# A recurrent block's GLA projections: fp32 products replaced by three fp16 products, with the weights split on POOL

## The reference

```python
xn = rmsnorm(x, ln1_w)                 # x is already layer-normed
q = xn @ Wq                            # 256 -> 128
k = xn @ Wk * scaling                  # 256 -> 128
gk = log_sigmoid(xn @ Wkg1 @ Wkg2 + bkg2) / 16   # 256 -> 16 -> 128
v = xn @ Wv                            # 256 -> 256
g = xn @ Wg + bg                       # 256 -> 256
...                                    # scan over tokens: S = S*exp(gk) + k v ; o = q S
x = x + (silu(g) * norm(o)) @ Wo
```

## Time and profile before

| | |
|---|---|
| median of three runs | 1288.07 us (1287.93 to 1289.17) |
| the profiled execution | 1286.95 us |
| its span in the profile | 1285.2 us |
| PE busy | 1127.8 us (88%) |
| DVE busy | 917.3 us (71%) |
| ACT busy | 691.5 us (54%) |
| POOL busy | 439.1 us (34%) |

### The profile page before, as it was taken

The page is one execution under the profiler, slowest core; times in us unless marked ns, Lnnn a source line. Parts: engine busy times, 40 slices in busy tenths (PEclk is TensorE's granted clock), DMA queues, the critical chain, the costliest instruction groups (busy, mean ns, idle before and its releaser), DMA issues. The chain is left out here.

```text
span 1285.2 us, 20632 instructions
## 1 busy us (share of the span) xinstructions
PE 1127.8 (88%) x6922; PEld 638.0 (50%) x6922; DVE 917.3 (71%) x1500; ACT 691.5 (54%) x1217; POOL 439.1 (34%) x253
## 2 busy tenths in 40 slices
PE   6866988999999899999997879756779999999997
PEld 4455855555555555555553754422344544444443
DVE  4978159999999899999995154799634155655554
ACT  3554267888777787777884124500554044344443
POOL 2821054444444354444220004254420033333331
PEclk9965988999999999999998987898879999999999
DMA  5243018887777787777779010400000344444331
GB/s 157 78 132 113 1 33 138 143 143 142 138 140 141 132 144 144 144 141 140 133 137 213 2 41 1 125 1 0 1 1 1 78 112 118 114 121 122 117 118 49
DMA packets 332820, 126.79 MB, mean 99 GB/s; under 512 B 273296, under 2 KB 328064, under 8 KB 332736
## 3 DMA queue, kind: packets, MB, share of 16 engines
q1 hardware_dynamic: 332736, 125.72, 45.6%
HBM read 57.26 MB, written 1.31 MB: 46 GB/s over the span
## 5 line engine op out<-in xcount | busy, mean ns | idle before, releaser
L1067 DVE SCALAR_TENSOR_TENSOR a_pr<-a_ex,a_rtot,a_pr 128x1024 f16<-128x1024 f32 x128 | 206.4, 1613 | 3.7 <-ACT a_pr L992 3.6
L848 POOL TENSOR_TENSOR a_rnorm<-a_ss,a_power 128x8 f32<-128x8 f32 x32 | 80.2, 2508 | 258.4 <-DVE a_ss L1033 258.3
L2058 POOL TENSOR_TENSOR e_sg<-e_sg,e_cb 128x512 f32<-128x512 f32 x64 | 82.0, 1282 | 242.1 <-ACT e_sg L2006 242.1
L1054 DVE TENSOR_REDUCE a_nmax<-psum 128x1 f32<-128x1024 f32 x128 | 155.4, 1214 | 12.9 <-PE psum L907 9.2
L984 ACT ACTIVATE a_ex<-psum,a_nmax 128x1024 f32<-128x1024 f32 x128 | 142.8, 1116 | 12.4 <-DVE a_nmax L1054 8.9
L992 ACT ACTIVATE a_pr<-a_ex,a_rtot 128x1024 f16<-128x1024 f32 x128 | 147.4, 1152 | 0.0
L889 PE MATMUL psum<-a_wh,xT_h 128*128 128x128 f16 (+1 forms) x512 | 115.3, 248 | 3.8 <-PEq L578 1.2
L2014 ACT ACTIVATE e_hh<-e_hf 128x512 f16<-128x512 f32 x64 | 40.3, 630 | 143.4 <-DVE e_hf L2083 143.4
L890 PE MATMUL psum<-a_wl,xT_h 128*128 128x128 f16 (+1 forms) x512 | 115.1, 248 | 0.0
L891 PE MATMUL psum<-a_wh,xT_l 128*128 128x128 f16 (+1 forms) x512 | 115.1, 248 | 0.0
L921 PE MATMUL psum<-a_pT,a_vh 128*128 128x512 f16 x256 | 98.2, 384 | 7.6 <-DMA a_pT<-a_pr 7.6
(11 more groups left out here) (349 smaller groups left out, 2706.8 us busy)
## 6 DMA issues: line engine op xcount, KB each, us to landing
e_cb<-comb_by_expert SPq DMA_DIRECT2D x64, 256.0 KB, 3.8
wf<-in_L_ffn_W_gate SPq DMA_DIRECT2D x32, 128.0 KB, 2.4
wf<-in_L_ffn_W_up SPq DMA_DIRECT2D x32, 128.0 KB, 2.4
wf<-in_L_ffn_W_down SPq DMA_DIRECT2D x32, 128.0 KB, 2.8
e_guf<-in_L_ffn_wg SPq DMA_DIRECT2D x32, 128.0 KB, 2.3
e_guf<-in_L_ffn_wu SPq DMA_DIRECT2D x32, 128.0 KB, 2.3
e_dnf<-in_L_ffn_wd SPq DMA_DIRECT2D x32, 128.0 KB, 2.1
a_wf<-in_L_attn_wq SPq DMA_DIRECT2D x16, 128.0 KB, 3.0
```

The lines of the kernel that those rows point to most:

```text
L1054: dve.tensor_reduce(nmax[:, k:k + 1], score_banks(m), AX.X, ALU.max, negate=True).then_inc(max_ready, 1)
L1067: dve.scalar_tensor_tensor(pr[k][:, 1, :], ex[e][:, :], rtot[:, e:e + 1], pr[k][:, 0, :], ALU.mult, ALU.subtract).then_inc(p_ready, 1)
```

## The change

The five projection weights are split into fp16 halves by POOL, in the block of the first norm (`side=split_weights`). For each weight POOL waits for its load, multiplies it by 64 in place, casts the high half and subtracts it to get the low half; `wv` is permuted in the same steps, chunk by chunk, which takes the place of L1508. The second norm now makes `xT_h` and `xT_l`. PE makes three fp16 products in place of each fp32 product of `wg1`, `wq`, `wk`, `wv` and `wg`, and waits for POOL's counts instead of the loads. The second gate product, the router's logits and all turns stay fp32. ACT and DVE divide by 64 where they read the sums.

```diff
-            xT = ptmp("xT", [P, DC, T])
+            xT_h, xT_l = ptmp("xT_h", [P, DC, T], F16), ptmp("xT_l", [P, DC, T], F16)
...
+            def split_weights(pool):
+
+                order = (("wg1", wg1, 2), ("wq", wq, 0), ("wk", wk, 1), ("wv", wv, 3), ("wg", wg, 4))
+                scaled = at = 0
+                for name, whole, i in order:
+                    pool.wait_ge(w_loaded[i], 16)
+                    high, low = halves[name]
+                    views = [(whole[:, :, :], high[:, :, :], low[:, :, :])]
+                    if name == "wv":
+                        views = [(whole[:, c, :].rearrange("p (h c d) -> p c d h", c=2, d=8),
+                                  *(x[:, c, :].rearrange("p (c d h) -> p c d h", c=2, d=8) for x in (high, low))) for c in range(DC)]
+                    scaled += 1
+                    pool.tensor_scalar(whole[:, :, :], whole[:, :, :], WSCALE, None, ALU.mult).then_inc(w_scaled, 1)
+                    pool.wait_ge(w_scaled, scaled)
+                    for f, h, l in views:
+                        at += 1
+                        pool.tensor_copy(h, f).then_inc(w_high, 1)
+                        pool.wait_ge(w_high, at)
+                        pool.tensor_tensor(l, f, h, ALU.subtract).then_inc(w_low, 1)
...
-            layer_norm(nc, env, "ln1", env["x"], xn, env["xnT"], interleaved=True, loads=load_first, stats=env["x1_stats"],
+            layer_norm(nc, env, "ln1", env["x"], xn, env["xnT"], interleaved=True, loads=load_first, stats=env["x1_stats"], side=split_weights,
...
-            rms_turned("g1_r1", xn, 0, xT, loads=load_rest)
+            rms_turned("g1_r1", xn, 0, xT_h, xT_l, loads=load_rest)
...
                     for c in range(DC):
-                        last = pe.matmul(psum[0:rows, banks + half, :], lhs(c), rhs_of(c, half),
-                                         start=(c == 0), stop=(c == DC - 1))
+                        pe.matmul(bank, wh[:, c, cols], xT_h[:, c, tokens], start=(c == 0), stop=False)
+                        pe.matmul(bank, wh[:, c, cols], xT_l[:, c, tokens], start=False, stop=False)
+                        last = pe.matmul(bank, wl[:, c, cols], xT_h[:, c, tokens], start=False, stop=(c == DC - 1))
...
-                    for i in range(len(loads) + 1):
-                        pe.wait_ge(w_loaded[i], 16)
+                    pe.wait_ge(w_loaded[5], 16)
+                    pe.wait_ge(w_low, 1)
...
-                    pool.wait_ge(w_loaded[3], 16)
-                    for c in range(DC):
-                        pool.tensor_copy(wv_dh[:, c, :].rearrange("p (c d h) -> p c d h", c=2, d=8),
-                                         wv[:, c, :].rearrange("p (h c d) -> p c d h", c=2, d=8)).then_inc(wv_ready, 1)
...
-                        dve.tensor_tensor(silu_g[:, n, :], psum[:, 4 + n % 2, 0:D], bg[:, :], ALU.add).then_inc(g_added, 1)
+                        dve.scalar_tensor_tensor(silu_g[:, n, :], psum[:, 4 + n % 2, 0:D], 1.0 / WSCALE, bg[:, :], ALU.mult, ALU.add).then_inc(g_added, 1)
```

More of the change, by code:

```diff
@@ L1428, in gated_linear_attention @@
             wv, wg, bg = ptmp("wv", [P, DC, D]), ptmp("wg", [P, DC, D]), ptmp("bg", [P, D])
-            wv_dh = ptmp("wv_dh", [P, DC, D])
-            wv_ready = sem("g1_wv")
+            halves = {name: [ptmp(f"{name}_{part}", [P, DC, width], F16) for part in "hl"]
+                      for name, width in (("wg1", G1), ("wq", KD), ("wk", KD), ("wv", D), ("wg", D))}
+            w_scaled, w_high, w_low = sem("g1_ws"), sem("g1_wh"), sem("g1_wv")
             loads = [(wq, w["L1_attn_Wq"]), (wk, w["L1_attn_Wk"]), (wg1, w["L1_attn_Wkg1"]), (wv, w["L1_attn_Wv"]),
@@ L1455, in gated_linear_attention, with both @@
             qk_done, act_done, dve_done, vh_done, g_added, v_free, x_high = (sem("g1_" + s) for s in ("qd", "ad", "dd", "vh", "ga", "vf", "xh"))
-            def both(pe, banks, lhs, rhs_of, rows=P):
+            def both(pe, banks, name, cols, rows=P):
+                wh, wl = halves[name]
                 for half in range(2):
+                    tokens, bank = slice(half * HALF, (half + 1) * HALF), psum[0:rows, banks + half, :]
                     for c in range(DC):
-                        last = pe.matmul(psum[0:rows, banks + half, :], lhs(c), rhs_of(c, half),
-                                         start=(c == 0), stop=(c == DC - 1))
+                        pe.matmul(bank, wh[:, c, cols], xT_h[:, c, tokens], start=(c == 0), stop=False)
+                        pe.matmul(bank, wh[:, c, cols], xT_l[:, c, tokens], start=False, stop=False)
+                        last = pe.matmul(bank, wl[:, c, cols], xT_h[:, c, tokens], start=False, stop=(c == DC - 1))
                 return last
@@ L1471, in _ @@
                     router.make_logits(pe)
-                    for i in range(len(loads) + 1):
-                        pe.wait_ge(w_loaded[i], 16)
[L1475 to L1479, removed]
+                    pe.wait_ge(w_loaded[5], 16)
+                    pe.wait_ge(w_low, 1)
+                    both(pe, 0, "wg1", slice(0, G1), G1).then_inc(mid_ready, 1)
+                    pe.wait_ge(w_low, 2)
+                    both(pe, 2, "wq", slice(0, KD)).then_inc(q_ready, 1)
+                    pe.wait_ge(w_low, 3)
+                    both(pe, 4, "wk", slice(0, KD)).then_inc(q_ready, 1)
                     pe.wait_ge(mid_done, 1)
@@ L1487, in _ @@
                     pe.wait_ge(qk_done, 1)
-                    pe.wait_ge(wv_ready, DC)
+                    pe.wait_ge(w_low, 3 + DC)
                     for cv in range(2):
-                        both(pe, 2 * cv, lambda c: wv_dh[:, c, cv * P:(cv + 1) * P], x_of).then_inc(v_ready, 1)
+                        both(pe, 2 * cv, "wv", slice(cv * P, (cv + 1) * P)).then_inc(v_ready, 1)
                     for n in range(NT):
@@ L1493, in _ @@
                             pe.wait_ge(qk_done, 2)
+                            pe.wait_ge(w_low, 4 + DC)
                         if n >= 2:
                             pe.wait_ge(g_added, n - 1)
+                        (wh, wl), tokens = halves["wg"], slice(n * P, (n + 1) * P)
                         for c in range(DC):
-                            last = pe.matmul(psum[:, 4 + n % 2, 0:D], xT[:, c, n * P:(n + 1) * P], wg[:, c, :],
-                                             start=(c == 0), stop=(c == DC - 1))
+                            pe.matmul(psum[:, 4 + n % 2, 0:D], xT_h[:, c, tokens], wh[:, c, :], start=(c == 0), stop=False)
+                            pe.matmul(psum[:, 4 + n % 2, 0:D], xT_h[:, c, tokens], wl[:, c, :], start=False, stop=False)
+                            last = pe.matmul(psum[:, 4 + n % 2, 0:D], xT_l[:, c, tokens], wh[:, c, :],
+                                             start=False, stop=(c == DC - 1))
                         last.then_inc(g_ready, 1)
@@ L1523, in _ @@
                     act.wait_ge(mid_ready, 1)
-                    act.activation(mid[:, :], psum[0:G1, 0:2, :].rearrange("p a b -> p (a b)"), ACT.Copy).then_inc(mid_done, 1)
+                    act.activation(mid[:, :], psum[0:G1, 0:2, :].rearrange("p a b -> p (a b)"), ACT.Copy,
+                                   scale=1.0 / WSCALE).then_inc(mid_done, 1)
                     act.wait_ge(q_ready, 1)
-                    act.activation(qT[:, :], two(2), ACT.Copy).then_inc(qk_done, 1)
+                    act.activation(qT[:, :], two(2), ACT.Copy, scale=1.0 / WSCALE).then_inc(qk_done, 1)
                     act.wait_ge(q_ready, 2)
-                    act.activation(kT[:, :], two(4), ACT.Copy, scale=float(GV) ** -0.5).then_inc(qk_done, 1)
+                    act.activation(kT[:, :], two(4), ACT.Copy, scale=float(GV) ** -0.5 / WSCALE).then_inc(qk_done, 1)
                     router.exponentials(act)
@@ L1540, in _ @@
                         act.wait_ge(v_ready, cv + 1)
-                        act.activation(v_h[:, cv, :], two(2 * cv), ACT.Copy).then_inc(vh_done, 1)
+                        act.activation(v_h[:, cv, :], two(2 * cv), ACT.Copy, scale=1.0 / WSCALE).then_inc(vh_done, 1)
                     router.turned(act)
```

2 lines of the change are left out of this document (1 added, 1 removed).

## The result

The kernel after takes 1294.27 us in the median of six runs (1291.89 to 1295.53), the kernel before 1288.0 in six runs beside it. The ratio is 1.0043 with a 95% interval of 1.003 to 1.0056, so the change costs 5.5 us (3.9 to 7.2). The forecast said 4.6 and slower, so sign and size were right. One of its terms was too small by 2.7, and an error of the other sign in another hid 0.7 of that.

The account below looks back on a forecast made before the run. It took PE to bound the projections, with each block's end a meeting of engines, so stage times add. First norm +6.0, second norm +2.8 and projections -4.2 gave +4.6 us, forecast 1292.7 us, range 1290.0 to 1296.3.

Parts of the forecast that it names:

- First norm: First norm's block: its end now waits for POOL, done at 774.0, so the next block starts 6.0 us later.
- it has one input, and I take that line: POOL's multiplications in the first norm's block: priced as one-input instructions, 0.18 us + 0.83 per thousand elements.
- my upper bound, the two-input price: First norm's block: five multiplications at the two-input price (+1.7) and waits twice as long give 8.5 us.
- rival 4: First norm's block: POOL slower than its rows, by the upper bound or collisions; sum 7.1, 1295.2 us; chance 10%.
- The collision that the prediction allowed for: First norm's block: at most one POOL instruction collides with DVE's scaling (L166), 0.3 us, inside the bounds.
- The exclusion that the prediction names: First norm's block: a single-input DVE instruction of this kind and a POOL instruction exclude each other; sum 0.3 higher.
- Second norm: Second norm ahead of the projections: making both halves lengthens the stretch from 7.05 to 9.89 us, +2.8.
- DVE joins the turn: Second norm ahead of the projections: with halves DVE takes part in the turn, +2.8 us, bounds 2.6 and 3.0.
- Projections: Projections' block: PE's own gain from fp16 products is 6.4 us, of which 4.2 arrives; bounds -6.4 and -2.5.
- The stall: Third tile of wg in the projections: PE waits about 2.1 us, once, for DVE's first bias addition.
- rival 2: Projections: the clock falls in PE's new wait, last tiles of wg at half pace, +1.7, 1294.4 us; chance 15%.
- Rivals 1, 3 and 5: In order: POOL not last in first norm, 1286.7, 8%; no wg wait, 1290.5, 5%; projection products no cheaper, 1297, 2%.

Follow-up runs that it names:

- the masks last: Kernel after with wk, wv, wg split later, four banks in both second norms, two biases first; POOL makes router halves before head masks: ratio 0.9951, 1280.86 us.
- two biases first: Kernel after, with DVE adding the first two biases of wg ahead of its step of the gate's chain: ratio 1.0053 against the kernel before, 1294.4 us.

## Why the prediction was right, and where it was not

**First norm, +8.66 against +6.0.** The mechanism held, point by point. POOL began 4.19 us after the block's start, against 4.05 by my rows, and the block ended with it. The failed step is "it has one input, and I take that line". The five multiplications took 0.38 + 0.85 + 0.85 + 1.49 + 1.49 = 5.06 us where I had 2.23, which is +2.83. Everything else came to its price: the six casts 2.82 against 2.82, the six subtractions 4.31 against 4.5, the gaps 0.63 against 0.6, the meeting 0.36 against 0.5. Even my upper bound, the two-input price, was too low (1.16 for 512 elements against 1.49), so the block's +8.66 lies above the bound of 8.5. This is rival 4, "POOL is slower than its rows", with a chance of 10%, and its sum of 7.1 is nearer to the 6.58 of the profile than the forecast's 4.6. Waits had no part in it, and a collision at most 0.2 us. The four permuted instructions took 0.60 and 0.78, and again 0.60 and 0.79, together 2.77, against my 2.9. The rule of the Trainium skill (GPSIMD Engine Reference, Performance pitfalls for Q7 kernels) had given 3.2: the subtractions come out near its 0.8, the casts lie 0.2 below it. What the casts do bear out is the step between its two figures, one cycle per element, 0.21 us for 256 elements as an estimate: they took 0.20 more than the plain cast's 0.40. The subtractions took only 0.11 more than a plain one's 0.67.

The collision that the prediction allowed for, up to 0.3 us, does show, on POOL's side. POOL's first multiplication began 0.21 us before DVE's scaling (L166) ended and itself ended 0.17 after it (766.11 + 0.38 against 763.65 + 2.67). In the nine profiles that have this pair it took 0.38 to 0.50 us and always ended 0.15 to 0.17 after L166. By the line through 0.85 and 1.49 it would take 0.29, an estimate, so the collision is worth 0.1 us here and 0.2 at most. The exclusion that the prediction names agrees with that. L166 takes 2.67 us for eight tiles in both kernels.

**Second norm, +2.84 against +2.8.** Taking it whole from the later norm gave the right number. "DVE joins the turn" holds for two banks only; with four the stage took 6.70, as the experiment showed.

**Projections, -4.92 against -4.2.** `wq` and `wk` took 5.28 (from 800.88 to 806.16), against 5.17. `wv` took 5.19, against 5.17. The stall came where I put it, at the third tile of `wg`, once, 1.70 against 2.1. `wg1` took 4.03 against 4.75: the clock rose 2.75 us into it and not 4.3. That is the term that was off: k came out 3.43 us earlier and not 2.83, and everything up to the first bias with it. Behind that, the first bias began 1.14 us after the start of the gate's step in place of the 1.36 that I had carried over from before; no run shows why. The moment of the clock is the one term I can't forecast, as `wg1` took between 3.9 and 5.0 over the kernels with fp16 products, and between 4.69 and 5.69 with fp32. The granted clock stayed at 1.00 through the stall (rival 2), as these windows of after show (window, us, busy of PE, PEld, DVE, ACT, POOL, granted clock, DMA):

```profile
812.00:814.00 2.00, 2.00 (x14) 1.23 (x13) 1.35 (x3) 1.97 (x3) 0.00 (x0) 1.00 0.00 0
814.00:816.00 2.00, 0.74 (x7) 0.41 (x5) 1.18 (x2) 0.79 (x1) 0.00 (x0) 1.00 0.00 0
816.00:818.00 2.00, 1.56 (x14) 1.30 (x15) 1.18 (x5) 1.59 (x2) 0.00 (x0) 1.00 0.02 4
```

Rivals 1, 3 and 5 fell: POOL was last, the stall came, and the products were cheaper.

**The sum.** An error of +2.7 in the first term and of -0.7 in the third left the profile 2.0 from the forecast, and the median, 5.5 us by the ratio, lies between. That the number was near is in part luck: errors of both signs met, and the other executions were less slow than the profiled one. Two figures don't come out of my own terms. The lower bound of the first term, 6.0 less 0.6 of gaps and five fixed parts of 0.18, is 4.5 and not 5.0. And the bounds as stated give a range of 1289.3 to 1296.9 (5.0 + 2.6 - 6.4 and 8.5 + 2.8 - 2.5 on 1288.07), where I had 1290.0 to 1296.3. The measured 1294.27 lies inside both.

## What to carry to other kernels

Work given to an idle engine is free only until the meeting at the block's end: ask when that engine is done, and put there what fits, here two of the five weights. Price an operation that the trace doesn't have by its own kind, or leave the bound open above the dearest row that you have. And before a new stage on a shared buffer is paid for, count the buffers: two more banks took the stage with halves from 9.89 us to 6.70, below the 7.05 of two banks without halves.

## What the runs showed of the hardware

- POOL's multiplication of fp32 by a constant took 0.85 us for 256 elements and 1.49 for 512, two times and more a cast's 0.40 and 0.61, and also more than a two-operand product with a broadcast column, 0.61 and 1.04.
- A DVE instruction that met one of POOL's was held until POOL's had ended. The copy of L201 met one in the block of the projections in all thirteen kernels and ended 0.03 to 0.05 us after it. The product of L1237 or L1238, with two inputs in SBUF, met one in four and ended 0.54 to 0.56 after it. Undisturbed, the copy of L201 takes 0.18 us, as the view of its line in the kernel before shows (smallest, median and largest ns of three):

```profile
L201 DVE COPY r_named<-r_best x3: 178/182/1561, 27.6 to 788.5; 128x32 f32<-128x32 f32 x2, 128x24 f32<-128x24 f32 x1
```

  The 1561 ns are those of the block of the projections: the copy ended at 790.04, POOL's subtraction at 790.00. With the masks last it took 4.50, over the subtraction and the memset behind it, and ended 0.04 us after that one. In the kernel before this was off the path, as DVE then waits 5.97 us for ACT (L1235); with the masks last it used up that slack, and L1235 starts without a wait. The order of the two matters: with the masks last L1237 began 0.02 us before POOL's mask and kept its 0.69, and the mask took 1.62 in place of 1.09. The Trainium skill, SBUF — State Buffer, section Who interferes with whom, has a copy that runs in a 2-port mode, and an instruction with two inputs in SBUF, among those of DVE that contend with POOL for a shared port; of the first it says that whoever issues first blocks the other for its whole instruction. The rows agree, and the 4.50 goes further, since the copy was held over a second POOL instruction too. They also agree on the exception: DVE's sum with one input in PSUM (L1231) took 0.69 beside POOL's subtraction in the kernel after.
- The same twelve products of `wg1` took between 3.92 and 4.97 us, as the clock rose at another place in them. A gain of under one us in this block must be read beside `wg1`'s time. Without it the block took 29.94 or 29.95 us in all five kernels with fp16 products and the old order of the biases, and 29.31 to 29.43 in the five profiles with two biases first.
